# Self-attention scores in sixteen 32x32 tiles over four banks, with the keys spread by group in place of the queries

## The reference

```python
q = (x @ w_q).reshape(B, S, N_HEAD, HEAD_DIM).transpose(0, 2, 1, 3)
k = (x @ w_k).reshape(B, S, N_KV_HEAD, HEAD_DIM).transpose(0, 2, 1, 3)
v = (x @ w_v).reshape(B, S, N_KV_HEAD, HEAD_DIM).transpose(0, 2, 1, 3)
q = _apply_rope(q); k = _apply_rope(k)
k = jnp.repeat(k, N_GROUP, axis=1); v = jnp.repeat(v, N_GROUP, axis=1)
attn = softmax(jnp.einsum('bhqd,bhkd->bhqk', q, k) * scale)
out = jnp.einsum('bhqk,bhkd->bhqd', attn, v).transpose(0, 2, 1, 3).reshape(B, S, D_MODEL)
return out @ w_o
```

## Time and profile before

| | |
|---|---|
| median of 3 runs | 803.13 us (801.89 to 804.63) |
| the profiled execution | 805.83 us |
| its span, first to last instruction | 803.8 us |
| mean granted clock of PE | 0.931 of full |
| self-attention stage | about 503 to 635 us of the span |

### The profile page before, as it was taken

How to read it: one execution, slowest core, us unless ns; L and a number is a source line. 1 busy time by engine, 2 the same in 40 slices (tenths; PEclk the granted TensorE clock), 3 DMA queues, 4 the chain that set the end, 5 groups by cost and what they waited for, 6 DMA issues and landing times.

```text
span 803.8 us, 27728 instructions
## 1 busy us (share of the span) xinstructions
PE 697.8 (87%) x9162; PEld 563.4 (70%) x9162; DVE 623.8 (78%) x1471; ACT 510.0 (63%) x1629; POOL 395.5 (49%) x409
## 2 busy tenths in 40 slices
PE   4735999999999999999999765899999689999485
PEld 2423776777777777777777644788888578889485
DVE  6415988999999999999999668489888756759621
ACT  2633876777777777777778524688888434545152
POOL 4730664544654455455463168477777310007275
PEclk9976999999999999999999969799999759999698
DMA  7596444444444444444340030000000000006980
GB/s 164 102 208 143 84 79 86 97 86 96 86 97 85 98 85 97 84 98 83 81 84 6 3 105 1 2 3 4 0 0 3 1 1 1 1 1 197 283 264 27
DMA packets 195179, 60.76 MB, mean 76 GB/s; under 512 B 147556, under 2 KB 193512, under 8 KB 195122
## 3 DMA queue, kind: packets, MB, share of 16 engines
q1 hardware_dynamic: 192000, 55.65, 31.5%
q0 software_dynamic: 1824, 3.96, 1.4%
q10 hardware_dynamic: 1298, 0.40, 0.2%
HBM read 51.58 MB, written 8.83 MB: 75 GB/s over the span
## 4 chain that ended last, share of the span: by engine, by line
PE 49%; SPq 16%; DVE 10%; issue 9%; ACT 7%; POOL 4%; ACTq 1%; DMA 1%; DVEq 0%; POOLq 0%
PE energy L487 22%; PE bank L487 15%; PE bank L490 13%; SPq L518 8%; ACT PR L650 6%; DVE X L1778 3%; DVE STAT L1512 2%; SPq L524 2%; POOL SX L947 1%; SPq L541 1%; SPq L566 1%; POOL TQ L939 1%; SPq L577 1%; SPq L568 1%; ACTq L650 1%
## 5 line engine op out<-in xcount | busy, mean ns | idle before, releaser
L650 ACT ACTIVATE PR<-energy,STAT 128x256 f32<-128x256 f32 x512 | 234.4, 482 | 113.2 <-DVE STAT L1512 113.2
L1512 DVE TENSOR_REDUCE STAT<-energy 128x512 f32 (+1 forms) x256 | 164.2, 684 | 26.4 <-PE energy L487 26.4
L490 PE MATMUL bank<-ident,PR 128*128 128x128 f32 x1024 | 152.9, 283 | 27.8 <-DVE PT L1529 23.0
L1529 DVE COPY PT<-bank 128x512 f32<-128x512 f32 x256 | 161.8, 670 | 1.4 <-PE bank L490 1.4
L490 PEld LDWEIGHTS bank<-ident,PR 128*128 128x128 f32 x1024 | 110.1, 142 | 58.6 <-issue 46.1
L845 POOL TENSOR_TENSOR QB<-QT,headmask 128x512 f32<-128x512 f32 x32 | 33.3, 1039 | 190.4 <-DMA MK<-in_mask_BxSxS_ik 120.0
L650 ACT ACTIVATION_READ_ACCUMULATOR PR<-energy,STAT (+1 forms) x512 | 110.2, 215 | 0.0
L852 POOL TENSOR_SCALAR MZ<-MK 128x512 bf16<-128x512 int32 x64 | 94.2, 1488 | 5.3 <-DMA MK<-in_mask_BxSxS_ik 5.3
L487 PEld LDWEIGHTS bank<-wv_s,CT 128*128 128x128 f32 x512 | 67.8, 194 | 31.7 <-issue 31.7
L487 PE MATMUL bank<-PT,VT 128*32 128x128 f32 x2048 | 69.5, 276 | 0.0
L487 PE MATMUL bank<-wv_s,CT 128*128 128x128 f32 x512 | 68.5, 277 | 0.3 <-DVE OC L1521 0.2
(11 more groups left out here) (270 smaller groups left out, 1361.6 us busy)
## 6 DMA issues: line engine op xcount, KB each, us to landing
CX<-in_ctx SPq DMA_DIRECT2D x512, 32.0 KB, 2.3
MK<-in_mask_BxSxS_ik SPq DMA_DIRECT2D x128, 128.0 KB
rows_in<-fill SPq DMA_DIRECT2D x1, 3483.0 KB, 19.6
X<-in_x SPq DMA_DIRECT2D x4, 512.0 KB, 7.7
VLT<-v_last SPq DMA_DIRECT2D x4, 512.0 KB, 9.0
QT<-in_L_ffn_W SPq DMA_DIRECT2D x16, 128.0 KB
OT<-in_L_ffn_W SPq DMA_DIRECT2D x16, 128.0 KB
PAY<-rows_in SPq DMA_DIRECT2D x2, 903.0 KB, 9.2
```

What stands on the lines that cost most here:

```text
L490: return nc.tensor.transpose(o, i, ident[0:n, 0:n])
L650: nc.scalar.activation(PR[:, b, g, :], EB[:, g, e * KEYS:(e + 1) * KEYS], ACT.Exp, bias=STAT[:, bass.ds(t, 1), b, 1, g:g + 1].rearrange("p ...
L1512: V.tensor_reduce(STAT[:, bass.ds(t, 1), b:b + 2, 1, g:g + 1].rearrange("p a b g -> p (a b g)"), EB[:, g, :].rearrange("p (e k) -> p e k", ...
L1529: V.tensor_copy(PT[:, k % 2, e, 2 * half:2 * half + 2, :].rearrange("p g k -> p (g k)"), psum[1 if e else 7]).then_inc(ev_t, 1)
```

## The change

The scores of one tile become 16 matmuls in place of 4: for each sequence b and each block h of 32 partitions, a stationary 32x32 piece of the rotated queries (straight from QKR) and a moving 32x128 piece of KB, written to the 32 partitions of sequence b in bank 2 + h. The tokens of the queries are then on the partitions, and the maximum and the sum run over the same 32 keys as before. KB is now the keys multiplied by the mask, made on POOL in `spread_keys`, where the queries were spread before; QD, `own_keys` on ACT and the KB memset on POOL go. The columns of the query weights are put in another order to match, and `weigh_values` reads SP at other places.

All four banks are used by each tile's scores, so `scores` waits for `shift_scores` of the tile before. `project` goes to bank 1 alone and waits for `rotary` of the tile before. On PE the waits of the scores are taken first (`await_scores`), then `project_out` is issued, then `scores`.

```diff
--- before.py
+++ after.py
@@ -377,7 +377,6 @@
         a_tq = sem("a_tq")
         a_qk = sem("a_qk")
         a_kb = sem("a_kb")
-        a_qd = sem("a_qd")
         a_s = sem("a_s")
         a_mx = sem("a_mx")
         a_sx = sem("a_sx")
@@ -748,20 +747,9 @@
                 wait_reuse(act, a_wo, t - 3)
                 nc.scalar.activation(SO[:, j, :], psum[7][:, 0:P], ACT.Copy).then_inc(a_so, 1)
 
-            def own_keys(t, j):
-
-                act.wait_ge(a_qk, t + 1)
-                wait_reuse(act, a_s, t - 3)
-                for g in range(NG):
-                    rows = slice(g * 32, g * 32 + 32)
-                    last = nc.scalar.activation(KB[rows, j, :, g, :],
-                                                QKR[rows, j, 1, :].rearrange("p (b k) -> p b k", b=BT), ACT.Copy)
-                last.then_inc(a_kb, 1)
-
-            act.wait_ge(zero_ok, 1)
             act.wait_ge(n1_shift, 1)
             centre(0, 0)
-            pipeline(act, [(5, evac_probs), (2, own_keys), (0, evac_xv), (1, evac_last_values), (3, exp_scores), (5, evac_o),
+            pipeline(act, [(5, evac_probs), (0, evac_xv), (1, evac_last_values), (3, exp_scores), (5, evac_o),
                            (-1, centre)], NT, 4, 6)
 
             act.wait_ge(n2_std, 1)
@@ -827,7 +815,6 @@
             nc.gpsimd.memset(zero_row[:, :], 0.0)
             nc.gpsimd.memset(fill[:, 0:ROW - 1], 0.0).then_inc(fill_ok, 1)
             nc.gpsimd.memset(fill[:, ROW - 1:ROW].bitcast(I32), NOWHERE).then_inc(fill_ok, 1)
-            nc.gpsimd.memset(KB[:, :, :, :, :], 0.0).then_inc(zero_ok, 1)
             nc.gpsimd.memset(sw_vg[:, :, :], 0.0).then_inc(zero_ok, 1)
 
             def norm_queries(u, h):
@@ -898,16 +885,17 @@
             tile(1, 1, False)
 
             pool.wait_ge(ld_s, N_S)
-            pool.wait_ge(zero_ok, 2)
+            pool.wait_ge(zero_ok, 1)
             nc.gpsimd.tensor_copy(digits[:, :, :].rearrange("p r k -> p (r k)"), digit_s).then_inc(wqk_ok, 1)
-            qv = sw_q[:, :].rearrange("p (h a f) -> p h a f", h=NG * 4, a=2)
+            qv = sw_q[:, :].rearrange("p (k g a f) -> p k g a f", k=NG, g=4, a=2)
             kv = sw_k[:, :].rearrange("p (k g a f) -> p k g a f", k=NG, g=1, a=2)
             for a in range(2):
                 for w, s in ((0, a), (1, 1 - a)):
-                    nc.gpsimd.tensor_copy(wqk[:, w, :].rearrange("p (h a f) -> p h a f", h=NG * 4, a=2)[:, :, a, :],
-                                          qv[:, :, s, :]).then_inc(wqk_ok, 1)
                     nc.gpsimd.tensor_copy(
-                        wqk[:, 2 + w, :].rearrange("p (k g a f) -> p k g a f", k=NG, g=4, a=2)[:, :, :, a, :],
+                        wqk[:, w, :].rearrange("p (g k a f) -> p k g a f", k=NG, g=4, a=2)[:, :, :, a, :],
+                        qv[:, :, :, s, :]).then_inc(wqk_ok, 1)
+                    nc.gpsimd.tensor_copy(
+                        wqk[:, 2 + w, :].rearrange("p (g k a f) -> p k g a f", k=NG, g=4, a=2)[:, :, :, a, :],
                         kv[:, :, :, s, :].broadcast_to([P, NG, 4, 4])).then_inc(wqk_ok, 1)
             for g in range(NG):
                 nc.gpsimd.tensor_copy(sw_vg[:, g, g * HD:(g + 1) * HD], sw_v[:, g * HD:(g + 1) * HD]).then_inc(wqk_ok, 1)
@@ -969,14 +957,14 @@
                 nc.gpsimd.tensor_tensor(QKR[:, j, :, :], TQ[:, j, 0::2, :], TQ[:, j, 1::2, :], ALU.add)\
                     .then_inc(a_qk, 1)
 
-            def spread_queries(t, j):
+            def spread_keys(t, j):
 
                 pool.wait_ge(a_qk, t + 1)
                 nc.gpsimd.tensor_tensor(
-                    QD[:, j, :, :, :],
-                    QKR[:, j, 0, :].rearrange("p (b a q) -> p b a q", b=BT, a=1).broadcast_to([P, BT, 4, SQ]),
-                    headmask[:, :].rearrange("p (a h c) -> p a h c", a=1, c=1).broadcast_to([P, BT, 4, SQ]),
-                    ALU.mult).then_inc(a_qd, 1)
+                    KB[:, j, :, :, :],
+                    QKR[:, j, 1, :].rearrange("p (b a q) -> p b a q", b=BT, a=1).broadcast_to([P, BT, NG, SQ]),
+                    headmask[:, :].rearrange("p (a h c) -> p a h c", a=1, c=1).broadcast_to([P, BT, NG, SQ]),
+                    ALU.mult).then_inc(a_kb, 1)
 
             def normalise_probs(t, j):
                 pool.wait_ge(a_inv, t + 1)
@@ -985,7 +973,7 @@
                     sinv[:, j, :].rearrange("p (n a) -> p n a", a=1).broadcast_to([P, 16, SQ]),
                     ALU.mult).then_inc(a_pn, 1)
 
-            pipeline(pool, [(2, rotate), (4, normalise_probs), (2, spread_queries)], NT, 4, 6)
+            pipeline(pool, [(2, rotate), (4, normalise_probs), (2, spread_keys)], NT, 4, 6)
 
 
             def input_rest(u, h):
@@ -1213,9 +1201,9 @@
 
             def project(t, j):
                 pe.wait_ge(a_xt, t + 1)
-                wait_reuse(pe, a_tq, 2 * t - 2)
+                wait_reuse(pe, a_tq, 2 * t)
                 for w in range(4):
-                    last = mm(psum[2 + j % 2][:, w * P:(w + 1) * P], wqk[:, w, :], xt[:, j, :])
+                    last = mm(psum[1][:, w * P:(w + 1) * P], wqk[:, w, :], xt[:, j, :])
                 last.then_inc(a_p, 1)
 
             def self_values(t, j):
@@ -1227,15 +1215,20 @@
                                   xt[:, j, b * SQ:(b + 1) * SQ], sw_vg[:, g, :])
                 last.then_inc(a_v, 1)
 
+            def await_scores(t, j):
+
+                pe.wait_ge(a_qk, t + 1)
+                pe.wait_ge(a_kb, t + 1)
+                wait_reuse(pe, a_sx, t)
+
             def scores(t, j):
 
-                pe.wait_ge(a_kb, t + 1)
-                pe.wait_ge(a_qd, t + 1)
-                wait_reuse(pe, a_sx, t - 1)
                 for b in range(BT):
-                    last = mm(psum[4 + j % 2][:, b * P:(b + 1) * P],
-                              QD[:, j, b, :, :].rearrange("p h q -> p (h q)"),
-                              KB[:, j, b, :, :].rearrange("p h q -> p (h q)"))
+                    for h in range(4):
+                        rows = slice(32 * h, 32 * h + 32)
+                        last = mm(EB[32 * b:32 * b + 32, h, 0:P],
+                                  QKR[rows, j, 0, b * SQ:(b + 1) * SQ],
+                                  KB[rows, j, b, :, :].rearrange("p g k -> p (g k)"))
                 last.then_inc(a_s, 1)
 
             def turn_probs(t, j):
@@ -1254,14 +1247,14 @@
                     for g in range(4):
                         last = mm(psum[7][32 * g:32 * g + 32, b * SQ:(b + 1) * SQ],
                                   XV[:, (j + 1) % 4, 1, b * SQ:(b + 1) * SQ],
-                                  SP[:, j, b, g * SQ:(g + 1) * SQ])
+                                  SP[:, j, g, b * SQ:(b + 1) * SQ])
                 last.then_inc(a_o, 1)
 
             def project_out(t, j):
                 pe.wait_ge(a_so, t + 1)
                 mm(psum[7][:, P:2 * P], SO[:, j, :], sw_o[:, :]).then_inc(a_wo, 1)
 
-            pipeline(pe, [(3, scores), (6, project_out), (1, project), (0, turn_x), (5, weigh_values),
+            pipeline(pe, [(3, await_scores), (6, project_out), (3, scores), (1, project), (0, turn_x), (5, weigh_values),
                           (1, self_values), (4, turn_probs)], NT, 4, 6)
 
 
@@ -1633,18 +1626,19 @@
                 for w in range(2):
                     V.tensor_tensor(
                         TQ[:, j, w::2, :].rearrange("p w (b s) -> p w b s", b=BT),
-                        psum[2 + j % 2][:, :].rearrange("p (w b s) -> p w b s", w=4, b=BT)[:, w::2],
+                        psum[1][:, :].rearrange("p (w b s) -> p w b s", w=4, b=BT)[:, w::2],
                         rope[:, w, :].rearrange("p (c d s) -> p c d s", c=1, d=1)
                         .broadcast_to([P, 2, BT, SQ]), ALU.mult).then_inc(a_tq, 1)
 
             def shift_scores(t, j):
                 dve.wait_ge(a_s, t + 1)
-                V.tensor_reduce(smx[:, j, :], psum[4 + j % 2][:, :].rearrange("p (n k) -> p n k", n=16), AX_X,
+                energy = EB[:, :, 0:P].rearrange("p h (g k) -> p h g k", g=NG)
+                V.tensor_reduce(smx[:, j, :].rearrange("p (h g) -> p h g", h=4), energy, AX_X,
                                 ALU.max).then_inc(a_mx, 1)
                 wait_reuse(dve, a_pt, t - 3)
                 dve.wait_ge(a_mx, t + 1)
-                V.tensor_tensor(SX[:, j, :, :], psum[4 + j % 2][:, :].rearrange("p (n k) -> p n k", n=16),
-                                smx[:, j, :].rearrange("p (n a) -> p n a", a=1).broadcast_to([P, 16, SQ]),
+                V.tensor_tensor(SX[:, j, :, :].rearrange("p (h g) k -> p h g k", h=4), energy,
+                                smx[:, j, :].rearrange("p (h g a) -> p h g a", h=4, a=1).broadcast_to([P, 4, NG, SQ]),
                                 ALU.subtract).then_inc(a_sx, 1)
 
             def sum_probs(t, j):
```

## The result

The changed kernel takes 812.03 us (median of 5 runs, 811.42 to 813.43), the kernel before 803.41 us (median of 5, 801.89 to 806.96). The ratio is 1.0104, 95% interval 1.0077 to 1.0131: slower by 8.6 us. Forecast were 812.5 us and slower by 9.4.

A forecast was written before the change was run, and what follows sets the result against it. Before, PE's own work and POOL's waits bound a step at 3.72 us; after, a ring of 4.10. 0.38 over 26 steps gives +9.9, stage ends -0.5: +9.4 us on 803.13, forecast 812.5 us, range 805 to 818.

The forecast's parts named there:

- project to the end of evac_o, with the exposed weight load: First part of the step: 3.13 us from project's first matmul to evac_o's end, plus 0.10 for an exposed weight load.
- evac_o's end to project_out: On PE, the delay from the end of evac_o on ACT to the start of project_out: 0.05 us.
- project_out to scores: On PE: 0.21 us to project_out's second pass, then 0.20 for the switch to the scores' tile shape.
- scores to project: On PE: 0.21 us from first to last start of 32 score records, then 0.20 to project's first 128x128 pass.
- the ring: Closed chain of waits: project, transpose, weigh_values, self_values, evac_xv, exp_scores, evac_o, project_out, project; 3.50 us, with scores entering 4.10.
- The reading that PE waited for ACT before the change: In one step before the change, PE issued project_out 0.05 us after evac_o ended; that step took 3.50 us.
- removing them only lengthens the wait, worth nothing: Four KB copies on ACT, 1.25 us a step, stand ahead of evac_xv, which waits for PE anyway: no gain forecast.
- the 3.13: Time in us from project's first matmul to evac_o's end in the kernel before, claimed untouched by the change.
- The ends of the stage: Self-attention's start and end: -0.4 us up to step 6 and about -0.1 in the last two steps.
- Banks, DVE's reads, POOL's product, clock: Fewer banks, DVE reading four banks, POOL's replaced product: each nothing; rival of a falling PE clock: 870 us, chance 0.03.
- The rival of hidden switches: On PE, tile-shape switches cost nothing, ring about 3.7 to 3.8 us; 803 to 805 us, chance 0.10.
- The rival of tiles that do not overlap: On PE, the scores' 32x32 tiles do not overlap fully; ring up to 4.78 us, 830 us, chance 0.08.

The follow-up runs named there:

- e1: The kernel before with project_out issued ahead of scores on PE, nothing else changed: 823.34 us, ratio 1.0245 to the kernel before.
- e2: The changed kernel with scores issued behind turn_probs and ahead of project_out, their waits taken before the last transpose of turn_probs: 803.35 us, ratio 0.9985 to the kernel before.
- e3: The changed kernel with evac_o ahead of evac_xv in ACT's queue: 798.57 us, ratio 0.9922 to the kernel before.
- e7: The kernel before with evac_o ahead of evac_xv in ACT's queue: 804.47 us, ratio 1.0011 to the kernel before.
- e9: The changed kernel with four 32x128 copies put back on ACT where own_keys stood: 814.95 us, ratio 1.0132 to the kernel before.
- e5: The kernel before with project in bank 1 alone, waiting for rotary of the tile before: 803.78 us, ratio 1.0002 to the kernel before.
- e4: The changed kernel with the 16 score matmuls issued twice in a row: 832.91 us, ratio 1.0347 to the kernel before.
- e8: e3 with spread_keys ahead of normalise_probs on POOL as well: 799.73 us, ratio 0.9955 to the kernel before.
- e6: The changed kernel with the edits of e2 and e3 together: 802.34 us, ratio 0.9975 to the kernel before.

## Why the prediction was right

The chosen mechanism held, and the time lies 0.5 us from the forecast. Its terms, against the changed kernel's step:

| term | forecast | measured, 575.91 to 579.97 |
|---|---|---|
| project to the end of evac_o, with the exposed weight load | 3.13 + 0.10 | 3.09 (575.91 to 579.00) |
| evac_o's end to project_out | 0.05 | 0.14 (579.00 to 579.14) |
| project_out to scores | 0.21 + 0.20 | 0.39 (579.14 to 579.53) |
| scores to project | 0.21 + 0.20 | 0.44 (579.53 to 579.97) |
| step | 4.10 | 4.06 |

The mean is 4.05, since every fourth step between 540 and 592 us, such as the one ahead of this, takes 4.00: 3.10 to the end of evac_o (575.01), then 0.05, 0.42 and 0.43.

- **PE's order and the ring: right**, shown by e1 (in), e2 (out) and e3 (shortened elsewhere). The prices on PE, all from rows of the kernel before, came out well: 0.39 to 0.42 and 0.43 to 0.44 us where 0.41 was forecast for each side of the scores, 0.23 for 0.21 from the first start of the burst to the last, and project's group lasts 1.16 us in place of 1.06 by the exposed load.
- **The reading that PE waited for ACT before the change: right, by 0.1 us.** The earlier trace rows have no idle time ahead of project_out at 577.91, for the scores fill PE until then; the reading rested on the 0.05 us behind evac_o. e7 bears it out: with evac_o early such steps take 3.40 us in place of 3.50.
- **ACT, "removing them only lengthens the wait, worth nothing": wrong in size.** The four copies cost the ring 0.13 us a step though ACT idled behind them, and their removal is what made evac_xv to exp_scores 0.28 for 0.41 (e9). I had counted the 3.13 as untouched by the change.
- **evac_o to project_out: too small**, 0.14 in most steps. I took the gap of one step, in which the scores filled PE until 0.05 us behind evac_o's end, as what the wait costs. The two errors have opposite signs, and so the sum is better than its terms: that the time lies within 0.5 us is in part luck.
- **The ends of the stage**: from project's first start to step 6 it is 1.0 us shorter (18.68 to 17.67), forecast 0.4; after step 32, to the last residual's end, 0.7 longer (15.42 to 16.15), forecast 0.1 shorter. Together -0.3 for -0.5, again by errors that cancel. With 26 steps of 0.337 the stage is 8.5 us longer, the medians 8.6. The two profiled executions are only 6.0 us apart, because project's first start came 2.4 us later in that of the kernel before (503.87, and 501.46 after); among the runs with that kernel's code it lies between 502.45 and 504.97, so this is scatter. The last residual in the profiles of before and after:

```profile
634.33 0.29 DVE L1661 TENSOR_TENSOR X<-X,bank 128x128 f32<-128x128 f32 x1 [1.70 <-PE bank L487]
```

```profile
640.40 0.29 DVE L1655 TENSOR_TENSOR X<-X,bank 128x128 f32<-128x128 f32 x1 [1.69 <-PE bank L486]
```

- **Banks, DVE's reads, POOL's product, clock: nothing, as forecast** (e5 for project's bank; 0.69 us for the reduction; clock 1.00 in the window with PE busy for 74.20 of 89 us). That the scores' own four banks cost nothing is read from the trace, where the wait ends 1.8 us early, and was not tried alone.
- **The rival of hidden switches falls**: 0.39 to 0.42 and 0.43 to 0.44 us on either side of the scores. **The rival of tiles that do not overlap falls** for this burst, with e4's limit: past 32 records the pace is 0.57 us for the next 32, 18 ns each. The Trainium skill (TensorE: Matmul & The Clock Gate, Part 3: Packing small matmuls) has about 4 ns from tile to tile; the runs show 7 ns for the first 16 records, and the section has no pace for a second burst over the same tiles.

What e3 left open was the next bound. e8 shows that the step stays at 3.59 us when one wait for POOL, for the keys, is exchanged for the other, for the probabilities.

## What to carry to other kernels

Before moving work in an engine's queue, write down each ring of waits that runs through it, with its length, not only the sums of the engines: work that is free in the shadow of a wait costs its full length on the other side of the instruction that waits (e1: 0.90 us of scores, a ring of 3.50 and then 4.40). If an edit lowers the busiest engine's sum and the time does not fall, look for the engine that now waits, follow its releaser back to itself, and move the link that need not stand in that queue (here evac_o, one name in a list, worth 13.5 us). A queue's idle time does not prove that what stands ahead of it is free.

## What the runs showed of the hardware that I had not expected

- 32x32 matmuls start 7 ns apart for the first 16 records and the first 32 start within 0.23 us; the next 32 of the same burst need 0.57 us (e4).
- Four ACT copies of 32x128 that nobody waits for, followed by 0.98 us of idle time, lengthen the distance between the next two activations from 0.28 to 0.41 us (e9). What in the engine does this stays open.
- PE stopped for 0.2 to 1.3 us, marked "issue", within bursts of small tiles in e2, e4, e6 and e8, and ahead of project in e3 (0.89 us). All of them lie in written-out steps or in the first round of the loop, so in instructions run for the first time. The cause was not tested.
